# Value product of an attention layer: float32 matmuls in two column halves of the array, in place of high and low float32r parts

## The reference

```python
dots = einsum('bhid,bhjd->bhij', q, k) * exp(temperature)
dots = where(eye, NEG_MAX, dots)
attn = softmax(dots, axis=-1)                   # 1024 x 1024 per head and batch
out  = einsum('bhij,bhjd->bhid', attn, v)       # the value product
```

## Time and profile before

| what | value |
|---|---|
| median of 3 runs | 554.29 us (553.81 to 554.71) |
| span of the profiled execution | 551.4 us, 2.9 us below that median |
| TensorE busy | 506.2 us, 92% |
| VectorE busy | 437.6 us, 79% |
| ScalarE busy | 392.5 us, 71% |
| GpSimd busy | 190.5 us, 35% |
| value matmuls | 1024, in 256 quarters |

### The profile page before, as it was taken

One profiled execution on the slowest core, in us unless ns is written; L12 is line 12 of the kernel. 1 busy time (PEld: TensorE's weight loads), 2 busy tenths in 40 slices (PEclk: granted clock), 3 DMA queues, 4 the chain that ended last, 5 costly groups with the idle time before them and its releaser, 6 DMA issues.

```text
span 551.4 us, 10337 instructions
## 1 busy us (share of the span) xinstructions
PE 506.2 (92%) x3466; PEld 406.8 (74%) x3466; DVE 437.6 (79%) x770; ACT 392.5 (71%) x690; POOL 190.5 (35%) x180
## 2 busy tenths in 40 slices
PE   0486999999999999999999999999999999976888
PEld 0362778888888888787888888888888888843434
DVE  0367599988898888888888888888889999795522
ACT  0115588888788788877887888778878887548575
POOL 1321243543433433343234343534353364440000
PEclk9969899999999999999999999999999999979999
DMA  6406705730762165251631652463257300000002
GB/s 219 187 2 139 174 2 111 181 76 27 175 140 76 43 157 116 77 124 39 129 101 42 160 116 78 94 156 66 76 124 181 88 1 1 1 1 1 1 9 68
DMA packets 32763, 49.10 MB, mean 89 GB/s; under 512 B 3418, under 2 KB 23636, under 8 KB 32468
## 3 DMA queue, kind: packets, MB, share of 16 engines
q1 hardware_dynamic: 32004, 47.75, 36.3%
q10 hardware_dynamic: 720, 0.85, 0.5%
HBM read 6.65 MB, written 1.05 MB: 14 GB/s over the span
## 4 chain that ended last, share of the span: by engine, by line
PE 81%; DVE 5%; ACT 4%; issue 4%; DMA 3%; POOL 1%; SPq 1%; DVEq 0%; POOLq 0%; ACTq 0%
PE ps L618 22%; PE ps L604 20%; PE ps L592 12%; PE ps L588 10%; PE ps L554 4%; PE ps L657 3%; DMA conv_sb<-in_conv 2%; ACT v_all L921 2%; ACT v_all L943 2%; PE ps L783 2%; PE ps L590 2%; PE ps L775 2%; PE ps L549 1%; PE ps L794 1%; DMA q_st<-arena 1%
## 5 line engine op out<-in xcount | busy, mean ns | idle before, releaser
L386 POOL TENSOR_SCALAR probs<-probs,inv_sum 128x1024 f32<-128x1024 f32 x128 | 144.0, 1125 | 262.0 <-DVE inv_sum L1164 262.0
L883 ACT ACTIVATE pt_hi<-ps 128x512 fp32r<-128x512 f32 x256 | 152.8, 598 | 56.8 <-PE ps L604 55.9
L1158 DVE TENSOR_TENSOR pt_lo<-ps,pt_hi 128x512 fp32r<-128x512 f32 x256 | 173.4, 682 | 13.0 <-ACT pt_hi L883 2.1
L1170 DVE TENSOR_REDUCE neg_max<-ps 128x1 f32<-128x1024 f32 x128 | 156.6, 1224 | 32.3 <-PE ps L592 31.4
L618 PE MATMUL ps<-pt_hi,v_slot 128*128 128x256 f32 x512 | 165.9, 346 | 0.5 <-DVE pt_lo L1158 0.5
L604 PE MATMUL ps<-ident,probs 128*128 128x128 f32 x1024 | 152.9, 272 | 0.6 <-DVE pt_lo L1158 0.6
L903 ACT ACTIVATE probs<-ps,neg_max 128x1024 f32<-128x1024 f32 x128 | 142.4, 1112 | 1.4 <-DVE neg_max L1170 0.7
L618 PE MATMUL ps<-pt_lo,v_slot 128*128 128x256 f32 x512 | 133.3, 282 | 0.0
L604 PEld LDWEIGHTS ps<-ident,probs 128*128 128x128 f32 x1024 | 123.2, 141 | 13.4 <-issue 0.9
L592 PE MATMUL ps<-k_lo,q_st 128*128 128x512 f32 x256 | 112.1, 438 | 0.0
L588 PE MATMUL ps<-k_hi,q_st 128*128 128x512 f32 x256 | 102.3, 399 | 5.3 <-DMA q_st<-arena 4.3
(11 more groups left out here) (127 smaller groups left out, 447.1 us busy)
## 6 DMA issues: line engine op xcount, KB each, us to landing
k_hi<-arena SPq DMA_DIRECT2D x32, 256.0 KB, 5.0
k_lo<-arena SPq DMA_DIRECT2D x32, 256.0 KB, 5.1
q_st<-arena SPq DMA_DIRECT2D x32, 256.0 KB, 3.7
v_slot<-v_all SPq DMA_DIRECT2D x16, 512.0 KB, 3.9
arena<-arena SPq DMA_DIRECT2D x28, 256.0 KB, 4.8
f_sb<-in_f SPq DMA_DIRECT2D x2, 1024.0 KB, 10.2
w_slot<-in_w_pairs SPq DMA_DIRECT2D x9, 128.0 KB, 2.1
x<-in_tok SPq DMA_DIRECT2D x2, 512.0 KB, 11.5
```

The source lines that it names most:

```text
L386: pool.tensor_scalar(probs[:, t % 4, :], probs[:, t % 4, :], inv_sum[:, t % 4:t % 4 + 1], 1.0, ALU.mult, ALU.mult).then_inc(norm_done, 1)
L883: act.activation(dst, ps[:, transposes_bank(t, a, drain), :].rearrange("p (j c) -> p j c", c=P), ACT.Copy).then_inc(hi_done, 1)
L1158: dve.tensor_tensor(pt_lo[at], ps[:, transposes_bank(t, a, drain), :].rearrange("p (j c) -> p j c", c=P), pt_hi[at].bitcast(F32), ALU.subt ...
L1170: dve.tensor_reduce(neg_max[:, t % 4:t % 4 + 1], ps[:, SCORES + 2 * (t % 2):SCORES + 2 * (t % 2) + 2, :].rearrange("p a c -> p (a c)"), AX ...
```

## The change

V and the probabilities are no longer split. `v_slot` holds 64 float32 columns per key tile, `pt` holds the probabilities as float32, and the value product is a float32 matmul with 64 stationary columns. Of the 8 key tiles, 0 to 3 are summed in columns 0 to 63 of the array (PSUM partitions 0 to 63) and 4 to 7 in columns 64 to 127; the existing sum of the two halves of a finished chunk now adds these. A quarter is one float32 matmul in each half. One bank of transposes is copied out by ScalarE, the other by VectorE, each in one operation. The low part of V and its VectorE operation fall away, and `v_all` is laid out by head, so that the load of a head moves half of the bytes. The two parts of the normalised input for the experts get a buffer of their own instead of lying in `pt_lo`.

```diff
-        v_all = sb("v_all", [P, NT, H, P], F32R)
-        v_slot = sb("v_slot", [P, 2, NT, P], F32R)
+        v_all = sb("v_all", [P, NT * H * P])
+        v_slot = sb("v_slot", [P, 2, NT, DH])
-        pt_hi = sb("pt_hi", [P, 2, NT, CW], F32R)
-        pt_lo = sb("pt_lo", [P, 2, NT, CW], F32R)
+        pt = sb("pt", [P, 2, NT, CW])
+        x2_parts = sb("x2_parts", [P, 2, SEQ], F32R)
+        v_heads = v_all[:, 0:H * NT * DH].rearrange("p (h t c) -> p h t c", t=NT, c=DH)
+        def pt_part(t, a):
+            m = (t - T_LAG) % SPH
+            return pt[:, m // 2 % 2, 4 * a:4 * a + 4, (m % 2) * P:(m % 2 + 1) * P]
...
             def head_v(h, k):
-                sp.dma_start(v_slot[:, k, :, :].bitcast(F32), v_all[:, :, h, :].bitcast(F32)
-                             ).then_inc(vs_loaded[k], 16)
+                sp.dma_start(v_slot[:, k, :, :], v_heads[:, h, :, :]).then_inc(vs_loaded[k], 16)
...
             def transposes(n, t, a, bank, begins):
...
                 if not begins:
-                    pe.wait_ge(lo_done, 2 * m - 1 + a)
+                    pe.wait_ge(pt_done[a], m)
...
             def values(chunk, c_local, slot, slot_loads, quarter, begins):
                 if quarter == 0:
-                    pe.wait_ge(lo_done, 4 * chunk + 4)
+                    for a in range(2):
+                        pe.wait_ge(pt_done[a], 2 * chunk + 2)
...
-                for jt in (2 * quarter, 2 * quarter + 1):
-                    for src in (pt_hi, pt_lo):
-                        ins = pe.matmul(ps[:, PV_BANK, 0:CW], v_slot[:, slot, jt, :], src[:, c_local % 2, jt, :],
-                                        start=jt == 0 and src is pt_hi, stop=jt == NT - 1 and src is pt_lo)
+                for a in range(2):
+                    jt = NT // 2 * a + quarter
+                    ins = pe.matmul(ps[DH * a:DH * (a + 1), PV_BANK, 0:CW], v_slot[:, slot, jt, :],
+                                    pt[:, c_local % 2, jt, :], start=quarter == 0, stop=quarter == 3,
+                                    tile_position=(0, DH * a))
...
 ScalarE, lagging:
-                for a in range(2):
-                    act.wait_ge(pt_ready, 2 * (n - T_LAG) + a + 1)
-                    act.activation(dst, ps[...], ACT.Copy).then_inc(hi_done, 1)
+                act.wait_ge(pt_ready, 2 * (n - T_LAG) + 1)
+                act.activation(pt_part(t, 0), ps[...], ACT.Copy).then_inc(pt_done[0], 1)
 VectorE, lagging:
-                for a in range(2):
-                    dve.wait_ge(hi_done, 2 * (n - T_LAG) + a + 1)
-                    dve.tensor_tensor(pt_lo[at], ps[...], pt_hi[at].bitcast(F32), ALU.subtract).then_inc(lo_done, 1)
+                dve.wait_ge(pt_ready, 2 * (n - T_LAG) + 2)
+                dve.wait_ge(pv_done, ...)
+                dve.tensor_copy(pt_part(t, 1), ps[...]).then_inc(pt_done[1], 1)
 VectorE, values (setup and work v0 to v7):
-            def low_values(t, bank):
-                return dve.scalar_tensor_tensor(v_all[:, t, :, DH:P], ps[...], v_scale, v_all[:, t, :, 0:DH], ...)
```

More of the change, by code:

```diff
@@ L191, in layer_kernel @@
         pt_ready = sem("pt_ready")
-        hi_done = sem("hi_done")
-        lo_done = sem("lo_done")
+        pt_done = [sem(f"pt_done{a}") for a in range(2)]
         pv_done = sem("pv_done")
@@ L246, in highs @@
         def highs(work):
-            return [x for x in order(work) if work[x][0] in "qkv"]
+            return [x for x in order(work) if work[x][0] in "qk"]
         USES = [4 + sum(len(w) for w in PAIR_WORK[:i]) for i in range(9)]
@@ L465, in _ @@
             weights(1)
-            sp.wait_ge(v_lo_done, NT)
+            sp.wait_ge(v_done, NT)
             head_v(0, 0)
@@ L736, in last_output @@
                 else:
-                    pe.wait_ge(lo_done, 2 * (B * SPB - 2))
+                    for a in range(2):
+                        pe.wait_ge(pt_done[a], B * SPB - 2)
                 project_output(o_slot[:, head, :], wo_last[:, head, :], c, bank).then_inc(work_mm, 1)
@@ L830, in high_qk, with scaled_values @@
                 return act.activation(dst, ps[:, bank, :], ACT.Copy)
-            def high_values(t, bank):
-                return act.activation(v_all[:, t, :, 0:DH], ps[:, bank, :].rearrange("p (h c) -> p h c", c=DH),
+            def scaled_values(t, bank):
+                return act.activation(v_heads[:, :, t, :], ps[:, bank, :].rearrange("p (h c) -> p h c", c=DH),
                                       ACT.Copy, scale=v_scale)
@@ L874, in lagging @@
                 idle = (fresh and t < T_LAG) or (drain and t >= T_LAG)
-                m_local = (t - T_LAG) % SPH
-                for a in range(2):
-                    if idle:
-                        break
-                    act.wait_ge(pt_ready, 2 * (n - T_LAG) + a + 1)
[L880 to L884, removed]
+                if idle:
+                    return
+                act.wait_ge(pt_ready, 2 * (n - T_LAG) + 1)
+                if not (fresh and t - T_LAG < 4):
+                    act.wait_ge(pv_done, pair.chunk0 + k * CPH + (t - T_LAG) // 2 - 1)
+                act.activation(pt_part(t, 0), ps[:, transposes_bank(t, 0, drain), :].rearrange("p (j c) -> p j c", c=P),
+                               ACT.Copy).then_inc(pt_done[0], 1)
             def output(pair, k, t, drain=False):
@@ L1066, in _ @@
                 low_qk(kind, SETUP_QK[kind]).then_inc(work_read, 1)
-            for t in range(NT):
-                dve.wait_ge(v_hi_done, t + 1)
-                low_values(t, 4 + t % 4).then_inc(v_lo_done, 1)
             def of_batch(a, b):
@@ L1130, in work @@
                 kind = pair.work.get((k, t))
-                if not kind or kind[0] in "ext":
+                if not kind or kind[0] in "extv":
                     return
@@ L1152, in lagging @@
                     return
-                m_local = (t - T_LAG) % SPH
-                for a in range(2):
-                    at = (slice(None), m_local // 2 % 2, slice(4 * a, 4 * a + 4),
-                          slice((m_local % 2) * P, (m_local % 2 + 1) * P))
-                    dve.wait_ge(hi_done, 2 * (n - T_LAG) + a + 1)
-                    dve.tensor_tensor(pt_lo[at], ps[:, transposes_bank(t, a, drain), :].rearrange("p (j c) -> p j c", c=P),
-                                      pt_hi[at].bitcast(F32), ALU.subtract).then_inc(lo_done, 1)
+                dve.wait_ge(pt_ready, 2 * (n - T_LAG) + 2)
+                if not (fresh and t - T_LAG < 4):
+                    dve.wait_ge(pv_done, pair.chunk0 + k * CPH + (t - T_LAG) // 2 - 1)
+                dve.tensor_copy(pt_part(t, 1), ps[:, transposes_bank(t, 1, drain), :].rearrange("p (j c) -> p j c", c=P)
+                                ).then_inc(pt_done[1], 1)
             def reciprocals(pair, k, t):
```

28 lines of the change are left out of this document (10 added, 18 removed).

## The result

The changed kernel takes **622.5 us** (median of 4 runs, 620.59 to 623.01) against 554.5 us in the same session: the ratio is 1.122, with a 95% interval of 1.118 to 1.126. It is 12% slower. 619.5 us was predicted, with a range of 603 to 633.

The account below looks back on a forecast made before the run. TensorE's instruction stream was taken to bound the steps; span 551.4 plus 67.8 for width changes, net of passes, less 2.5 for copies gave 616.7, plus 2.9 to the median: 619.5 us, range 603 to 633.

Parts of the forecast that it names:

- TensorE's stream alone sets the time: In the steps TensorE's instruction stream has no hole and alone sets the time; ScalarE and VectorE have slack.
- Passes: 0.43 instead of 0.47 per quarter: Value product: the two column halves overlap, so a quarter's passes cost 0.43 us, 0.04 less than before.
- A change of width costs 0.15 in, 0.16 out to transposes, 0.20 out to scores: At each quarter's edges the array is emptied (0.10 us each way) and a weight load exposed (0.05, 0.06 or 0.10).
- the forecast's two pairs: Way in plus way out of a quarter: 0.31 us toward transposes, 0.35 toward scores.
- hidden in the stream: Rival at the four edges per step: narrow weight loads start under wide matmuls, so the kernel gets faster, 542 us; 6%.
- Half of the edges hidden: Rival at the step's edges: only the emptying or only the exposed loads are paid, 577 to 594 us; 5%.
- +0.54 us per plain step: Plain step of 3.43 us instead of 2.89: +0.25 for the quarter before transposes, +0.29 for that before scores.
- The copies give 2.5 us: Fewer copies save TensorE waits: about 1.2 us in the first steps, 0.7 between 449 and 457, 0.6 in the drain.
- The sum: Whole span: 551.4 + 67.8 - 2.5 = 616.7 us, with the runs' median 2.9 above the span.

Follow-up runs that it names:

- experiment 8: Changed kernel with both matmuls of a quarter in the same column half, so nothing can overlap: 729.0 us, ratio 1.318.
- experiment 1: Changed kernel with both quarters of a step together after the first bank of transposes, two changes of width per step instead of four: 578.1 us, ratio 1.044.
- experiment 2: Changed kernel with both quarters together at the end of the step, ahead of the scores: 583.6 us, ratio 1.052.
- experiment 7: Changed kernel with float32 value matmuls at full width, v_slot 128 wide with zeros in the upper 64 columns, no halves: 649.8 us, ratio 1.174.
- experiment 4: Kernel before, with a chunk's four quarters together after the first bank of transposes in every second step: 586.2 us, ratio 1.059.
- experiment 6: Kernel before, with a chunk's four quarters together at the end of every second step: 572.9 us, ratio 1.033.
- experiment 10: Kernel before plus one tiny bfloat16 matmul of zeros per quarter, 128 stationary columns, so no change of width: 584.9 us, ratio 1.057.

## Why the prediction was right, point by point

- **TensorE's stream alone sets the time.** Right. ScalarE lost 67 us of busy time and VectorE 82, and it bought 1.7 us, as told below; the sum of TensorE's starts explains the rest.
- **Passes: 0.43 instead of 0.47 per quarter, with the halves side by side.** Right: the records come in twos, and experiment 8 took the overlap away and paid 106.5 us, where 110 was the price.
- **A change of width costs 0.15 in, 0.16 out to transposes, 0.20 out to scores.** Right, and shown three ways: experiment 1 saved 44.4 us for 44 forecast (in, and out to scores), experiment 2 38.9 for 39 (in, and out to transposes), and experiments 7 and 8 gave 0.31 for a pair, where the mean of the forecast's two pairs is 0.33. The rival *hidden in the stream* falls with experiments 1 and 7. *Half of the edges hidden* falls with the idle time before loads on both sides of each quarter.
- **+0.54 us per plain step.** 3.45 - 2.89 = 0.56 measured. A step forecast at 3.43 came out at 3.45. Over all steps the growth is 0.55 on average, some 1 us more than forecast in all.
- **The copies give 2.5 us.** The places were right, one size was not: the starts in the two traces show about 1.7 us. Between 449 and 457 the step that starts at 453.56 took 3.97 us and its counterpart (519.18) 3.86, where the steps around them grew by 0.55: 0.66 of the 0.7. TensorE had waited there 0.47 for VectorE ahead of L686, and does so no more. In the drain the quarter that started 1.11 after its transposes (473.44 to 474.55) now starts 0.64 after them (541.35 to 541.99), with 0.35 and 0.58 as the usual distances: 0.7, where 0.6 was forecast. In the first steps only one gained, 0.29 (4.81 to 4.53, from 69.20), where 1.2 was forecast: this term was too large. No run changed the copies alone.
- **The sum.** The span was forecast at 616.7 and is 620.7, 4.0 us more. The starts of the matmul group of the scores are, in the kernel before and after (ns min/median/max, first and last start):

```profile
L588 PE MATMUL ps<-k_hi,q_st x256: 386/394/803, 54.9 to 468.0; 128*128 128x512 f32 x128
```

```profile
L590 PE MATMUL ps<-k_hi,q_st x256: 387/473/796, 56.1 to 535.3; 128*128 128x512 f32 x128
```

  Between first and last, 479.2 stands against 413.1, 66.1 more. The forecast has 122 steps at 0.54 there, less 1.9 for the copies, 64.0: about half of the difference is the 0.01 per step, the other half the copies. Another 1.2 us lies ahead of the first score matmul, and 0.8 of the 2.0 behind the last one were not forecast. Both are stretches in which TensorE's granted clock was at its lower level in the one execution and not in the other. In the setup the 24 records of L532 (L534) took 4.0 us before and 5.1 after, at a granted clock of 0.64 and 0.51; behind the last step the transposes and products from L710 (L714) on took 2.56 us (497.18 to 499.74) and 3.91 (565.08 to 568.99), at 1.00 and 0.57, after TensorE had waited for VectorE in both; a stretch ahead of these gave back 0.4. The stretches are 29 to 35 us before and after, then those of L710 and L714 (us, busy of each engine, clock, DMA):

```profile
29.00:35.00 6.00, 5.59 (x32) 5.59 (x32) 5.70 (x29) 0.17 (x1) 2.12 (x2) 0.64 0.01 1
```

```profile
29.00:35.00 6.00, 5.48 (x26) 5.48 (x26) 5.75 (x29) 0.16 (x1) 2.12 (x2) 0.51 0.01 1
```

```profile
497.18:499.80 2.62, 2.62 (x15) 1.81 (x15) 2.62 (x5) 1.42 (x3) 0.00 (x0) 1.00 0.00 0
```

```profile
565.08:569.00 3.92, 3.92 (x15) 3.48 (x16) 3.35 (x6) 1.44 (x3) 0.00 (x0) 0.57 0.00 0
```

  The change need not be the cause of the first: over the profiled executions of all experiments the first score matmul starts anywhere from 53.6 to 55.8 us with the setup of the kernel before and from 54.3 to 56.5 with that of the changed one. The median of the runs lies 1.8 us above the span, not 2.9. In all later executions of the kernel before it is 1.7 or 1.8 as well, so the execution behind the forecast was by that about 1.1 us shorter than the median, and this hid as much of the 4.0: that the total missed by only 3.0 is in this part luck.

The Trainium skill, TensorEngine Tiling (Array Packing), section Tiling Modes, says under Key Properties that a change of tiling mode drains TensorE. The traces agree: experiments 1, 7 and 8 show it with 0.31 to 0.35 us for a narrow stretch, reloading included.

**No better version was found.** With column halves a narrow stretch must carry enough passes to pay for its two edges: a quarter saves 0.04 us, the edges cost 0.31 to 0.35, so by this estimate eight or nine quarters in one stretch break even. Four in one stretch, as many as one chunk has, give 561. Eight would take the values of two chunks at once and buffers for four; that was not tried, and experiments 4 and 6 say what an uneven order does to the rest.

## What to carry to other kernels

When a matmul is put on part of the columns, count how often TensorE goes from full width to part width and back: here each stretch cost 0.31 to 0.35 us, three quarters of the 0.43 us of work in it. Put the narrow matmuls together before you judge the change, and run the same order in the old kernel as a control, since order alone moved it by 19 to 32 us; but the new kernel need not lose as much by it. Where one engine sets the time, work that is taken from the others is worth little: here 150 us of it bought 1.7. And a busy share of TensorE near 100% says nothing about such gaps; they show as idle time before weight loads that waited for nothing, and the starts of the matmuls give their price.

## What the runs showed of the hardware that was not expected

- A tiny bfloat16 matmul at full width, 64 columns long, costs the stream 0.12 us per use between float32r matmuls (experiment 10: 30.9 us over 256), four times its share of the 0.12 that 256 columns take (0.03, an estimate). The next matmul starts 0.03 after it, and the one after that 0.21 later and not 0.12, so most of the cost is the load behind it. The kernel before has the same at L590 in every step: 0.04 to the score matmul behind it, which takes 0.31 to the transposes at 154.22, where a score matmul takes 0.23 elsewhere:

```profile
153.87 0.23 PE L590 MATMUL ps<-ident_b,neg_diag 128*128 128x128 bf16 x1
153.91 0.48 PE L592 MATMUL ps<-k_lo,q_st 128*128 128x512 f32 x1
```

- Two float32 column halves overlap fully also where each accumulates over four matmuls into its half of one PSUM bank (0.416 of 0.43 us per quarter).
- TensorE's granted clock falls to the lower of its two levels in stretches of the setup and behind the last step, and where these lie differs from one execution to the next: by it the same 24 records (L532, L534) took 4.0 us in one and 5.1 in the other.
